# Another order of the expert loop's tiles on all engines, and of its weight and bias loads

## The reference

```
x = x + linear_attention(layernorm(x), Wq, Wk, Wv, Wo)      # 16 heads, elu + 1
x = x + cross_attention(layernorm(x), ctx, ctx)             # l2-normalised q, k; one k*v vector per sample
x = x + ffn(layernorm(x))

ffn(x): xn = layernorm(x) * gamma + beta
        top2 of softmax(xn @ Wg.T) over 8 experts -> two gates per token
        y = sum over experts e of gate_e * (gelu(xn @ W1[e] + b1[e]) @ W2[e] + b2[e])
        return x + y
```

## Time and profile before

| | |
|---|---|
| median of 3 runs | 491.24 us |
| lowest, highest | 489.79, 495.32 us |
| profiled execution | 486.6 us |
| its span | 484.5 us |
| TensorE busy | 427.4 us, 88% |
| VectorE busy | 358.3 us, 74% |
| ScalarE busy | 322.0 us, 66% |
| GpSimd busy | 241.1 us, 50% |
| moved by DMA | 79.60 MB, mean 164 GB/s |

### The profile page before, as it was taken

One profiled execution on the slowest core, in us unless ns is written; L12 is line 12 of the kernel. 1 busy time (PEld: TensorE's weight loads), 2 busy tenths in 40 slices (PEclk: granted clock), 3 DMA queues, 4 the chain that ended last, 5 costly groups with the idle time before them and its releaser, 6 DMA issues.

```text
span 484.5 us, 8783 instructions
## 1 busy us (share of the span) xinstructions
PE 427.4 (88%) x2929; PEld 381.8 (79%) x2929; DVE 358.3 (74%) x839; ACT 322.0 (66%) x635; POOL 241.1 (50%) x349
## 2 busy tenths in 40 slices
PE   0799999999999998997999997999799897989770
PEld 0577887878787785896999997989699797989660
DVE  1635657776767888986999697888888787978850
ACT  2455565657656476967985978876879686785730
POOL 2223446465565658586946554734533553522331
PEclk9999999999999997998999999999999999999996
DMA  8900020202020336545288787878877889776621
GB/s 277 303 0 32 15 66 24 65 25 65 25 67 22 112 141 237 185 172 166 95 227 252 225 252 249 261 240 261 299 237 255 269 243 314 224 256 208 164 27 16
DMA packets 32464, 79.60 MB, mean 164 GB/s; under 512 B 4674, under 2 KB 23746, under 8 KB 26532
## 3 DMA queue, kind: packets, MB, share of 16 engines
q1 hardware_dynamic: 23456, 67.94, 40.8%
q0 software_dynamic: 7488, 10.39, 10.8%
q10 hardware_dynamic: 1476, 0.72, 0.5%
HBM read 69.40 MB, written 9.63 MB: 163 GB/s over the span
## 4 chain that ended last, share of the span: by engine, by line
PE 38%; DMA 16%; ACT 13%; DVE 12%; POOL 9%; issue 8%; SPq 1%; ACTq 0%; DVEq 0%; POOLq 0%
PE bank L401 23%; DMA w1r<-ff_ 9%; DMA y_<-yb,idxs 6%; ACT hf L1120 4%; PE bank L631 3%; PE bank L408 3%; ACT w2h L914 3%; POOL y_ L1987 2%; PE bank L638 2%; ACT w1h L904 2%; ACT xf L1090 1%; DVE w2l L1612 1%; PE bank L672 1%; PE bank L565 1%; ACT hh L1128 1%
## 5 line engine op out<-in xcount | busy, mean ns | idle before, releaser
L1987 POOL DMA_INDIRECT y_<-yb,idxs x29 | 52.9, 1825 | 102.1 <-DVE yb L1664 73.8
L401 PE MATMUL bank<-w2h,hh 128*128 128x256 f32 x312 | 89.0, 285 | 9.5 <-DVE ya L1657 9.5
L401 PE MATMUL bank<-w2l,hh 128*128 128x256 f32 x312 | 87.5, 280 | 0.0
L401 PE MATMUL bank<-w2h,hl 128*128 128x256 f32 x312 | 87.4, 280 | 0.0
L401 PE MATMUL bank<-xh,w1h 128*128 128x256 f32 x256 | 74.7, 292 | 2.3 <-issue 0.9
L904 ACT ACTIVATE w1h<-w1r 128x1024 fp32r<-128x1024 f32 x46 | 48.5, 1058 | 39.1 <-DMA w1r<-ff_ 38.4
L401 PE MATMUL bank<-xl,w1h 128*128 128x256 f32 x256 | 72.9, 285 | 0.0
L401 PE MATMUL bank<-xh,w1l 128*128 128x256 f32 x256 | 72.8, 284 | 0.0
L401 PEld LDWEIGHTS bank<-w2h,hh 128*128 128x128 f32 x312 | 59.1, 189 | 11.0 <-issue 10.9
L1364 DVE TENSOR_TENSOR w1l<-w1r,w1h 128x1024 fp32r<-128x1024 f32 x46 | 55.7, 1222 | 15.3 <-ACT w1h L904 15.3
L1612 DVE TENSOR_TENSOR w2l<-w2r,w2h 128x1024 fp32r<-128x1024 f32 x46 | 55.8, 1221 | 4.8 <-ACT w2h L914 4.4
(11 more groups left out here) (251 smaller groups left out, 1046.0 us busy)
## 6 DMA issues: line engine op xcount, KB each, us to landing
w1r<-ff_ SPq DMA_DIRECT2D x23, 1024.0 KB, 8.4
w2r<-ff_ SPq DMA_DIRECT2D x23, 1024.0 KB
b1r<-b_ SPq DMA_DIRECT2D x7, 512.0 KB
bs<-ff_ SPq DMA_DIRECT2D x23, 132.0 KB
xn_rows<-xn SPq DMA_DIRECT2D x8, 264.0 KB, 2.3
xin<-x_ SPq DMA_DIRECT2D x8, 256.0 KB, 6.7
cT<-ctxT_ SPq DMA_DIRECT2D x8, 256.0 KB, 3.6
cin<-ctx_ SPq DMA_DIRECT2D x8, 256.0 KB, 3.8
```

Of the source, the lines that this page charges most:

```text
L401: r = e.matmul(o, a_(t), b_(t), start=first and m == 0, stop=m == n - 1)
L1987: e.indirect_dma_start(out=out[:, :], out_offset=bass.IndirectOffsetOnAxis(ap=at, axis=0), in_=yb[t % 2][:, i, :], in_offset=None, compute ...
```

## The change

The loops over the tiles from 5 on are written anew on SP, TensorE, ScalarE and VectorE. GpSimd's is not touched. Tiles of three sorts now have orders of their own: half tiles, full tiles behind a half tile, and full tiles behind a full tile (with tile 5 as a special case of these). The set of calls is the same.

```diff
@@ SP
             load_w2(4)
+            load_w1(5)
             load_b(4)
             for t in range(5, NT):
-                load_w1(t)
+                if t + 1 < NT:
+                    load_w1(t + 1)
+                load_w2(t)
                 load_b(t)
-                load_w2(t)
@@ TensorE
-            for t in range(5, NT + 1):
...
+            for t in range(5, NT):
+                if KIND[t] == "H":
+                    layer1_half(t, 0)
+                    layer1_half(t, 1)
+                    if t + 1 < NT:
+                        xpose(t + 1)
+                    layer2(t - 1, 0)
+                    turn(t)
+                    layer2(t - 1, 1)
+                elif KIND[t - 1] == "H":
+                    layer1(t, 0)
+                    layer1(t, 1)
+                    xpose(t + 1)
+                    layer1(t, 2)
+                    layer1(t, 3)
+                    layer2(t - 1, 0)
+                else:
+                    if t > 5:
+                        xpose(t + 1)
+                    layer1(t, 0)
+                    layer1(t, 1)
+                    if t == 5:
+                        xpose(t + 1)
+                    layer1(t, 2)
+                    layer2(t - 1, 0)
+                    layer1(t, 3)
+                    layer2(t - 1, 1)
+            layer2(NT - 1, 0)
@@ ScalarE
+                if KIND[t] == "H":
+                    w2_high(t, 0)
+                    if t + 1 < NT:
+                        w1_high(t + 1, 0)
+                        w1_high(t + 1, 1)
+                    gelu_half(t, 0)
+                    gelu_half(t, 1)
+                    if t + 1 < NT:
                         x_affine(t + 1)
+                    w2_high(t, 1)
+                    turned_high(t, 0)
+                    turned_high(t, 1)
+                    continue
+                if t > 5 and KIND[t - 1] == "F":
+                    x_affine(t + 1)
+                w1_high(t + 1, 0)
+                w1_high(t + 1, 1)
...
+                w2_high(t, 0)
+                w2_high(t, 1)
+                gelu(t, 0)
...
+                if t == 5 or KIND[t - 1] == "H":
+                    x_affine(t + 1)
+                gelu(t, 1)
+                gelu(t, 2)
+                h_high(t, 0)
+                gelu(t, 3)
+                h_high(t, 1)
@@ VectorE
+                if KIND[t] == "H":
+                    add_bias(t, 0)
+                    add_bias(t, 1)
...
+                elif KIND[t - 1] == "H":
+                    w1_low(t + 1, 0)
+                    w2_low(t, 0)
+                    w1_low(t + 1, 1)
+                    x_split(t + 1)
+                    w2_low(t, 1)
                     h_low(t, 0)
+                    h_low(t, 1)
+                    weigh(t - 1, 0)
+                else:
+                    w1_low(t + 1, 0)
                     x_split(t + 1)
+                    w1_low(t + 1, 1)
                     w2_low(t, 0)
+                    weigh(t - 1, 0)
                     w2_low(t, 1)
+                    h_low(t, 0)
+                    weigh(t - 1, 1)
+                    h_low(t, 1)
+            weigh(NT - 1, 0)
```

More of the change, by code:

```diff
@@ L868, in tensor @@
             layer2(3, 1)
-            for t in range(5, NT + 1):
-                half = t < NT and KIND[t] == "H"
-                for q in range(2 if half else 4):
-                    if half:
-                        layer1_half(t, q)
-                    elif t < NT:
-                        layer1(t, q)
-                    if q == 1 and t + 1 < NT:
-                        xpose(t + 1)
-                for i in range(ROWS[t - 1]):
-                    layer2(t - 1, i)
-                    if half and i == 0:
-                        turn(t)
+            for t in range(5, NT):
[3 more added lines that the diff above has]
+                    if t + 1 < NT:
+                        xpose(t + 1)
+                    layer2(t - 1, 0)
[20 more added lines that the diff above has]
+            layer2(NT - 1, 0)
         def scalar(e):
@@ L1738, in vector @@
             weigh(3, 1)
-            for t in range(5, NT + 1):
-                half = t < NT and KIND[t] == "H"
-                for c in range(2):
-                    if half:
-                        add_bias(t, c)
-                    if t + 1 < NT:
-                        w1_low(t + 1, c)
-                if t < NT and not half:
+            for t in range(5, NT):
+                if KIND[t] == "H":
+                    add_bias(t, 0)
+                    add_bias(t, 1)
+                    if t + 1 < NT:
+                        w1_low(t + 1, 0)
+                    w2_low(t, 0)
+                    if t + 1 < NT:
+                        w1_low(t + 1, 1)
+                        x_split(t + 1)
+                    weigh(t - 1, 0)
+                    w2_low(t, 1)
+                    turned_low(t, 0)
+                    turned_low(t, 1)
+                    weigh(t - 1, 1)
+                elif KIND[t - 1] == "H":
+                    w1_low(t + 1, 0)
+                    w2_low(t, 0)
+                    w1_low(t + 1, 1)
+                    x_split(t + 1)
+                    w2_low(t, 1)
                     h_low(t, 0)
-                if t + 1 < NT:
+                    h_low(t, 1)
+                    weigh(t - 1, 0)
+                else:
+                    w1_low(t + 1, 0)
                     x_split(t + 1)
-                if t < NT:
+                    w1_low(t + 1, 1)
                     w2_low(t, 0)
+                    weigh(t - 1, 0)
                     w2_low(t, 1)
-                    if half:
-                        turned_low(t, 0)
-                        turned_low(t, 1)
-                    else:
-                        h_low(t, 1)
-                for i in range(ROWS[t - 1]):
-                    weigh(t - 1, i)
+                    h_low(t, 0)
+                    weigh(t - 1, 1)
+                    h_low(t, 1)
+            weigh(NT - 1, 0)
         RS = {}
```

21 lines of the change are left out of this document (4 added, 17 removed).

## The result

| | median, us | runs |
|---|---|---|
| before | 491.4 | 489.8 to 495.3 (4) |
| after | 463.1 | 461.6 to 464.8 (4) |

The ratio is 0.941, with a 95% interval of 0.935 to 0.948. The forecast was 471.0, with 467 to 482: the sign and the mechanism were right, the gain of 28 us is 8 more than the 20 forecast, and the time lies outside the range. The profiled execution took 464.1 us (before 486.6).

What follows compares the result with a forecast made beforehand. Bound: TensorE's own time plus waits from one late 1 MB load (w1). 20.7 us of waits and 1.1 at the end go, 1.8 return with `b1r`: profiled execution 466.6, plus 4.6 carried over, 471 us; range 467 to 482.

Steps and rivals of the forecast that it cites:

- the margins: Half tiles: inputs ready ahead of TensorE by 1.7 us at the turn, 1.0 before layer 2, 1.6 for xl.
- w1 loads 14 us or more ahead of their reader: Sign on SP: w1 loads issued at least 14 us before their first reader, and taking less time to land.
- The bias of tile 4: Load now behind w1(5): ScalarE slips 2 us, covered on TensorE, cost zero; 2 us once if the cover were gone.
- the path through the GELU of the half tile: On ScalarE the GELU stood behind the late w1, so TensorE's turns waited, 7.1 us in 7 waits.
- the 4.6 us carried over: Median of runs 491.2 lay 4.6 us above the profiled execution of 486.6; the same was added to the forecast.
- the 20.7 us of waits: TensorE's waits in the expert loop: 9.5 us before layer 2, 7.1 at turns, 4.1 before layer 1; all go.
- the 1.8 us for `b1r`: Cost of the bias load moved back: 0.6 us on each of tiles 12, 17, 22, with 0 to 4.2 in all.
- The end: After the last matmul: tile 21's rows weighed earlier, so the last scatters go sooner; gain 1.1 us, 0 to 1.5.
- The scatter chain: On GpSimd each tile's scatter starts only when the previous tile's has landed; taken as no cost.
- L: Time of a scatter from issue to landing; taken as 5 to 8 us, must be under 8.2 or somewhat more.
- B: Rival, chance 0.08: the scatter chain binds; 476 to 477 us at L = 9.0, 486 at 9.5.
- D: Rival, chance 0.06: slower, since a late scatter goes through VectorE straight to TensorE; 496 us at L = 10.1.

Runs made afterwards that it cites:

- SP alone: The kernel before with only SP's load order changed (w1 one tile further ahead, bias load last), all engines in the old order: 468.1 us, ratio 0.959.
- GELU first: The kernel before with both add_bias first on VectorE and both gelu_half first on ScalarE in half tiles, loads unchanged: 491.3 us, ratio 1.0005.
- engines alone: The changed kernel with SP's loads in the old order, so only TensorE, ScalarE and VectorE are reordered: 473.6 us, ratio 0.971.
- bias behind w2: The kernel before with one line of SP's loop moved, the bias load after w2 of its tile: 475.9 us, ratio 0.975.
- late entry: The changed kernel with the loads for tiles 4 to 6 in the old order, w1 one tile ahead only from tile 7 on: 465.5 us, ratio 0.952.
- the extra load: The changed kernel with 448 KB more to load per tile from tile 5 on, into a buffer nobody reads: 468.0 us, ratio 0.955.
- the old order on TensorE: The changed kernel with TensorE's loop alone in the old order; SP, ScalarE and VectorE new: 465.2 us, ratio 0.948.
- bias-first kernel: The changed kernel with the bias load ahead of w2 of its tile again, w1 still one tile ahead: 465.4 us, ratio 0.957.

## Why the prediction was right in kind and short in size

**The bound, the cause and the margins** held. TensorE was the engine, the late w1 was the cause (SP alone: ScalarE's waits for w1 0, 21.3 us gained), and the waits of the earlier trace rows went all together. The margins came out as worked out: 1.7 us at the turn, `h_low` 2.2 us after the start of the half tile. One sign failed: I had asked for w1 loads 14 us or more ahead of their reader, and only 5 of the 17 are (9.8 to 17.2 us, 12 in the middle). It did no harm, so 14 was more than was needed; whether they also land faster no profile shows. VectorE at 90% in the loop did not become the bound. The bias of tile 4 went behind w1(5), and no wait on TensorE came of it.

**One link was drawn too narrowly.** I followed the path through the GELU of the half tile. The kernel with the GELU first shows that to open this path alone moves the wait to the next layer 1. The sum survived because the change removed what was late, not only that path.

**The step that failed is the sum.** Its path was right, and three of its terms were mis-sized: the 4.6 us carried over from profile to median came out as -1.0 (5.6 off, the largest), the 20.7 us of waits as 24.7 (4.0 off), the 1.8 us for `b1r` as 0. A later start of the loop, 3.2 us, and 0.2 at the end went the other way, which makes the 8 us. Had the start not been later, the forecast would have been 11 us off: that it was only 8 is luck.

**The waits term, 20.7 us.** By starts of matmuls the loop is 207.7 us before and 183.0 after, 24.7 less. The list of waits counts each from the end of the matmul before it, and in the earlier trace rows that end is 0.28 us after its start while the next start would have been 0.12 after it: 292.23 to 293.54 is 1.31 us, of which 1.19 are lost, and the list says 1.03. So 0.16 us is missing a wait; about as much again goes where the next group starts slowly or two turns run apart that now run as one (1.04 us for eight). The window of the earlier trace rows hides part of it: it ends at 465.8, one layer-2 row and one wait short of the last matmul at 470.4; the list of waits did run to the end. The other profiles say the same:

| profile | waits in the loop by the list | loop over 183.0 | over the list, per wait |
|---|---|---|---|
| before | 20.7 in 16 | 24.7 | 0.25 |
| SP alone | 2.9 in 5 | 4.0 | 0.22 |
| engines alone | 9.4 in 9 | 13.4 | 0.44 |
| bias behind w2 | 7.8 in 10 | 12.3 | 0.45 |
| GELU first | 20.3 in 15 | 26.0 | 0.38 |

In the last three the granted clock of the loop is 0.99, so a slow stretch of some 1.5 us is in them too; without it they come to 0.28 to 0.30 a wait.

**The `b1r` term, 1.8 us back,** did not come: `add_bias` never waits for it. I had put 0.6 us on each of three tiles between 0 and 1.4, with no row that showed a delay; 0, the lower end, is what happened.

**The 4.6 us carried over** were the largest error. The profile shown was at the low end of before: five of its spans have a mean of 486.8 against 484.5. The median of the first runs, 491.2, was at the high end: all 60 runs of before have a median of 489.6, and all 20 of the changed kernel 463.1, so that of the 28.3 us measured first 26.4 are left. And what lies above the profile is in part caused by the waits (the slow stretches), so that part goes with them. After, the median lies 1.0 us *under* the profiled execution; in the repetitions it lies 0.2 to 2.5 under. I had treated as a constant of the program what was chance of one profile and one set of runs and in part a property of the kernel before.

**The end** gained 0.9 us (from the last matmul to the end of the span 14.1 before, 13.2 after) of the 1.1 forecast. Three further profiles of the changed kernel have 13.3, 13.3 and 15.2, the four of before 14.4.

**A cost that I did not have:** the loop starts 3.2 us later, 265.9 against 262.7. Of this 1.7 is a wait of xpose(5) for the gather of tile 5 (by starts it loses 1.9 us there, and 0.2 before); 1.5 is that TensorE reaches xpose(5) later, at 257.9 and not 256.3, and that is within the scatter of the first part (256.3 to 259.0 in the five profiles of before, 254.9 to 259.8 in the four of the changed kernel). These four start the loop at 264.7 to 267.7 and wait 1.6 to 1.9 us for the gather; the five of before start at 262.7 to 265.5, with no such wait in the list. In the changed kernel w1(6) is issued at 252.17, beside that gather (its first issue 253.08), where before SP issues nothing between 247.88 and 255.52. With the old order of these loads (late entry) the wait is gone and the loop starts at 263.1, but w1 is late in it. The stretch from the gather's first issue to xpose(5), before and in the changed kernel, the last two columns the DMA share and GB/s:

```profile
252.10:256.50 4.40, 4.39 (x37) 4.19 (x35) 4.37 (x9) 4.13 (x10) 3.45 (x4) 1.00 0.66 128
```

```profile
253.00:259.76 6.76, 5.03 (x42) 4.83 (x42) 6.61 (x10) 5.52 (x11) 4.79 (x4) 1.00 1.06 336
```

After, the gather shares DMA engines that have no room left. All profiles with xpose(5) in its place sort the same way. Over the 4.5 us from that gather's first issue, the DMA share is 0.63 to 0.69 in eight (the five of before, the orders alone, the bias behind w2, the late entry): xpose(5) comes 4.4 to 4.5 us after the issue, and no wait is listed. The share is 0.96 to 1.09 in the nine others, and all of them wait. In six xpose(5) comes 6.0 to 6.7 us after the issue and has waited 1.6 to 1.9. In the other three (the extra load, the old order on TensorE, the GELU first) it comes 7.9 to 9.0 after it and has waited 8.1 to 9.3, since TensorE was at its place early, at 250.9 to 252.8, before the gather was issued at all. The kernel with the GELU first has the old loads, but in its profile SP issued w2 and w1 at 253.19 and 254.63, beside a gather at 253.29. So loads beside the gather go with a slower gather in every profile, and with the loads moved away (late entry) it is fast; why TensorE was early in three stays open.

The parts add up for the profiled execution: 466.6 - 4.0 (waits) - 1.8 (`b1r`) + 0.2 (end) + 3.2 (start) = 464.2, measured 464.1. The median is 463.1 instead of that plus 4.6. The 3.2 is what this one execution had; the bias-first kernel has the same wait (1.7) and starts its loop at 263.1.

**The range** was too narrow below for the same reason: its lower end took all waits as gone but at the list's size. The costs that I knew had two ends, the gain had one.

**The scatter chain.** No cost, as taken, but by less margin than taken: L was 6.9 to 9.3 us, where I had 5 to 8 and a threshold near 8.2 for every tile. My 10.1 was also not the one busiest row of before: four scatters in its loop that a later one waited for have 8.9 to 10.8 us, the longest from 393.54 to 404.32. "If GpSimd waits mostly for its own scatters, B or D is right" was wrong: it does (46.0 us in 12 waits), VectorE waits 2.8 us behind it, and TensorE not at all. An engine that waits for its own work has become the bound only when TensorE waits for it in the end. On the rule of taking turns (the Trainium skill, DMA: Bandwidth & Descriptors, Queues, rings and completion order), from which I had an estimate of 9.0 us for a scatter beside loads: the loop's 6.9 to 9.3 lie below it or close to it, the 10.1 and 10.8 of before above, so here it is no upper bound; and the 5 us that I tied to it did not come. The kernel with the extra load, with 7.5 to 9.9 us at a DMA share of 1.00, shows that there was still room.

## What to carry to other kernels

A large load whose buffer is free must not stand in the issuing queue behind a small one whose gate opens late (here 13.4 us for one line); look at what each gate waits for, in order, before looking at bandwidth. Where one late item reaches the bound engine by several in-order queues, closing one path moves the wait and gains nothing: take away the lateness. And price the waits of a saturated engine by the starts of its instructions, with and without the wait, over the whole stretch, not by the list (24.7 us against 20.7 here); then take more than one profile of the kernel before for the base.

## What was not expected of the hardware

- A 1 MB load took 7.4 us from issue to its reader behind one bias load and `b1r`, and 9.2 in the burst of the earlier trace rows; at a share of 1.00 the DMA engines moved 340 GB/s for 100 us beside a TensorE that was never idle.
- Waits of 1.4 to 2.3 us on TensorE were followed in two of five executions of the same kernel by stretches at the lower clock (0.64 over 4.7 us in one), 1.5 us dearer, and not in the other three, which have waits up to 2.1 us too.
- A small indirect gather with 1 MB loads beside it (DMA share 0.96 to 1.09) was read 6.0 to 9.0 us after its issue in nine executions of nine; with the DMA engines at 0.63 to 0.69 4.4 to 4.5 us after it in eight of eight.
